# Latent attention taken four sequences at a time, values moved inside a loop, and filler matrix products before the norms of an eight-stage tower

## The chip, the cores and the metric

The kernel runs on one core of one Trainium2 chip. The metric is the device time of one execution in microseconds (us). Engines are named as the profile names them: PE is TensorE (matrix products), PEld its weight loads, DVE VectorE, ACT ScalarE, POOL GpSimd, SP the engine that here only issues DMAs. "PEq" and the like are an engine's own sequencer, mostly a barrier.

## The reference, cut to what matters

32 images become 32 sequences of 37 tokens of 256 features, and eight stages follow. Each stage is normalised first; the stages touched here are the first attention (L0_attn), the last one (latent attention, in L3_ffn), and the norms of all stages.

```
# L3_ffn, latent attention: 16 heads of 64, of which 32 without and 32 with rotation
q = (x @ Wq).reshape(b, t, H, D).transpose(0, 2, 1, 3)
ckv = x @ Wkva
kv_latent, k_rope = (ckv[:, :, :R], ckv[:, :, R:])
kv = (kv_latent @ Wkvb).reshape(b, t, H, NOPE).transpose(0, 2, 1, 3)
...
att = jnp.einsum('bhqd,bhkd->bhqk', q, k) / jnp.sqrt(jnp.float32(D))
att = jnp.where(mask, att, jnp.float32(-jnp.inf))
att = jax.nn.softmax(att, axis=-1)
y = jnp.einsum('bhqk,bhkd->bhqd', att, v)
# L0_attn, 16 heads of 16
out = jnp.einsum('bhqk,bhkd->bqhd', attn, V).reshape(B, S, H * dv)
```

A token attends only to earlier tokens of its own sequence.

## The kernel before

1184 tokens lie in 11 tiles of 111 rows (three sequences each; the last tile has two), `h` [111, 11, 256]. Each stage is one or more blocks. In a block each engine has its own program, written out in order; the engines meet only at semaphores, and at a barrier at the block's end, which also waits until an engine has issued all its DMAs. The order of the work is the order in which it is written; no planner sets it.

**Norms.** `norm_dve` (or `norm_transpose`) forms mean and variance of 11 tiles on DVE, POOL the power -0.5, DVE and ACT the normed tiles. PE waits for these (`norm_turn`, L1321; in `norm_transpose` L188) and turns them with 22 transposes into PSUM, from where ACT and DVE copy them into `xT`. Nine norms have such transposes: ap (attention 0), g, e, sn, mn, dn, de, lp (latent attention), le.

**Attention 0** (`stage_attn0`, L428). A first block forms queries, keys and values. Values leave PE in six pieces (L565). ACT copies queries to `qm` (16 copies, L607), then the values to `vt` (L614), and SP moves `vt` to `vx` by 24 DMAs (L505): 12 for tiles 0 to 3 once two pieces are there, 12 for the rest. A second block loops over 22 half-tiles: scores, softmax, transposes, mixing with `vx`, output.

**Latent attention** (`latent_attention`, L3704). The first block folds weights on PE (L3779), norms, and forms keys and eight query blocks as nine jobs: PE (L3797), ACT out of PSUM (L3839, L3841), DMA swap, and three DVE operations for the rotation (L3900, L3895, L3896). After job 4, eleven transposes give the values `lat` by tiles of 111 rows (L3811, copied at L3859 and L3861). The second block loops over 22 units of one tile (three sequences) and eight heads. The scores of a unit are 111x111 for each head, so two thirds of them join tokens of different sequences and are masked by `neg` [111, 111]. In steady state, for unit u:

- PE: 8 products of scores (L3936), 4 of mixing unit u-3 (L3959), 2 of the output of unit u-4 (L3970), 8 transposes of unit u-2 (L3948).
- DVE: mask added on the way out of PSUM (L4038), maximum (L4043), its negative times the scale (L4045); reciprocal of the sums and product with it (L4053, L4055); every second unit the output added to `r` (L4062).
- ACT: 8 exponentials with the maximum as bias and the sum as a second output (L3995), 2 copies of turned weights (L4007), 1 of mixed values (L4017).

A product of fp32 operands goes to PE as two instructions, a transpose as one. So 24 instructions are 12 products.

Of the kernel before, what the change touches and what calls it, by code (L numbers as in the profile page):

```python
# [15 lines left out]
ALU = mybir.AluOpType  # L16
# [7 lines left out]
P = 128  # L24
B, S, D = 32, 37, 256
G = 3
# [69 lines left out]

def norm_transpose(nc, name, h, xT, ident, eps, center, w_dram=None, w_plus=0.0, x_tok=None, turn=True,
# [5 lines left out]
    with ExitStack() as stack:  # L103
# [84 lines left out]
        def _(pe):  # L188
            for g, (a, b) in enumerate(groups):
# [238 lines left out]
def stage_attn0(nc, d, h, xT, ident):  # L428
# [7 lines left out]
    with ExitStack() as stack:  # L436
# [6 lines left out]
            "loop_in k_in v_in0 v_in1 v s_mm sc max exp norm turned pT mix oT out h").split()))  # L443
# [9 lines left out]
        bo = sb("a_bo", [1, D])  # L453
        ones = sb("a_ones", [1, TT])
        k_dram = nc.dram_tensor("a_kd", (D, G * SEQ), F32, kind="Internal").ap()

        with ExitStack() as inner:
# [10 lines left out]
            vt = sb2("ap_vt", [TT, NT, 2, NP, 2, 16])  # L468
# [8 lines left out]
            def _(sp):  # L477
# [22 lines left out]
                for m, (lo, hi) in enumerate(((0, 4), (4, NT))):  # L500
                    sp.wait_ge(n["values"], 2 if m == 0 else 6)
                    for q in range(G):
                        for a in range(2):
                            for x, y in ((0, 32), (32, S)):
                                sp.dma_start(  # L505
                                    vx[a * S + x:a * S + y, lo:hi, q, :, :].rearrange("j t p x -> j t (p x)"),
                                    vt[q * S + x:q * S + y, lo:hi, a, :, :, :].rearrange("j t p b x -> j t (p b x)")
                                ).then_inc(s[f"v_in{m}"], 16)

            @block.gpsimd  # L510
            def _(pool):
# [6 lines left out]
                nc.gpsimd.memset(vt[:, :, :, :, :, :], 0.0).then_inc(n["zero_v"], 1)  # L518

# [60 lines left out]
            def _(act):  # L580
# [20 lines left out]
                act.wait_ge(n["zero_q"], 1)  # L601
                for c in range(KC):
                    act.wait_ge(n["qu"], NCH * (c + 1))
                    for p in range(4):
                        for q in range(2):
                            dst, src = moved(c, p, q)
                            nc.scalar.activation(dst, src, ACT.Copy)  # L607
                act.wait_ge(n["zero_v"], 1)
                for m in range(6):
# [50 lines left out]
        with ExitStack() as inner:  # L660
# [3576 lines left out]
```

## Time and profile before

| | |
|---|---|
| three runs | 2040.03, 2045.87, 2044.94 us, median 2044.94 |
| the profiled execution | 2042.88 us, of which the span 2041.0 us |
| busy: PE, PEld, DVE, ACT, POOL | 71%, 56%, 72%, 42%, 30% |
| granted TensorE clock, mean | 0.84 of full |

The span lies between the first and the last instruction; 1.9 us lie around it. The granted clock is 1.00 (2.4 GHz) or 0.50 (1.2 GHz); means lie between. Where an engine's row says "idle before", the arrow names what ended the idle time.

### The profile page before, as it was taken

How to read it: one execution, taken by the hardware profiler on the slowest of the kernel's cores; microseconds unless marked ns; L12 is line 12 of the kernel's file. 1: busy time of each engine (PE TensorE's matmuls, PEld its weight loads, DVE VectorE, ACT ScalarE, POOL GpSimd, SP SyncE). 2: the span in 40 equal slices, each digit the busy share in tenths (PEclk: the TensorE clock that was granted, in tenths of full speed). 3: DMA queues.
4: the chain of work that ended last, by engine and by line, in shares of the span. 5: the costliest groups of instructions: out<-in, count | busy, mean ns of one | idle time of the engine just before them, and what ended most of it. 6: DMA issues, size and time to landing. Idle time of an engine off the chain costs nothing. (4 is left out here: it accounts for less than half of the span.)

```text
span 2041.0 us, 23929 instructions
## 1 busy us (share of the span) xinstructions
PE 1440.9 (71%) x8142; PEld 1134.0 (56%) x8142; DVE 1460.6 (72%) x2433; ACT 866.2 (42%) x1905; POOL 602.6 (30%) x395
## 2 busy tenths in 40 slices
PE   3678222469997825787657970797768889778797
PEld 3466101359997412344346970795347779556687
DVE  7566777898665459999945753687976466789576
ACT  5456230355552344554412530673233243369532
POOL 1400002122220028999805305125212141100310
PEclk9888555779999868898967995799889979889799
DMA  3410100111100003422045612101343010310110
GB/s 94 102 29 2 42 0 0 50 48 42 42 1 29 0 3 141 131 63 69 0 151 128 186 58 49 27 19 36 103 124 83 19 39 16 81 25 1 40 32 25
DMA packets 65583, 108.80 MB, mean 53 GB/s; under 512 B 34684, under 2 KB 43927, under 8 KB 63850
## 3 DMA queue, kind: packets, MB, share of 16 engines
q1 hardware_dynamic: 57725, 93.44, 15.7%
q0 software_dynamic: 6176, 8.84, 2.2%
q10 hardware_dynamic: 1562, 5.00, 0.8%
q8 instruction: 65, 1.06, 0.2%
q14 instruction: 55, 0.45, 0.1%
HBM read 83.85 MB, written 18.13 MB: 50 GB/s over the span
## 5 line engine op out<-in xcount | busy, mean ns | idle before, releaser
L2478 PE MATMUL c_pc<-c_st,ident 128*128 128x407 f32 x384 | 157.0, 559 | 49.4 <-POOL c_st L2441 42.2
L2433 POOL TENSOR_TENSOR c_dbub<-c_dub,c_bcb 128x814 f32<-128x814 f32 x96 | 169.5, 1788 | 16.4 <-DMA c_bcb<-s_bc 9.4
L2417 ACT ACTIVATE c_da<-s_delta,s_a 128x407 f32<-128x407 f32 x192 | 108.1, 594 | 115.1 <-DVE c_st L2525 100.2
L2478 PEld LDWEIGHTS c_pc<-c_st,ident 128*128 128x128 f32 x384 | 77.2, 208 | 127.7 <-POOL c_st L2441 59.0
L2521 DVE TENSOR_TENSOR_SCAN c_da<-c_da,c_dbub 128x814 f32<-128x814 f32 x60 | 110.6, 1843 | 1.7 <-POOL c_dbub L2433 1.7
L2019 ACT ACTIVATE e_sg<-e_pu,e_b 128x444 f32<-128x444 f32 (+1 forms) x96 | 56.6, 590 | 80.1 <-PE e_pu L1945 74.5
L2100 DVE TENSOR_TENSOR e_sg<-e_sg,e_gate 128x444 f32<-128x444 f32 (+1 forms) x96 | 54.7, 570 | 47.9 <-ACT e_sg L2019 44.7
L3172 DVE SCALAR_TENSOR_TENSOR dc_acc<-dc_pp,dc_cw,dc_acc 128x1311 f32<-128x1311 f32 x48 | 75.9, 1584 | 17.1 <-ACT dc_acc L3105 15.2
L1907 POOL TENSOR_TENSOR e_wlb<-e_wb,e_whb 128x1024 fp32r<-128x1024 f32 x16 | 42.1, 2657 | 125.8 <-ACT e_whb L1994 125.8
L2707 POOL DMA_INDIRECT me_xe<-m_xs,mt_rowsb x48 | 48.2, 1003 | 77.4 <-DVE mt_rowsb L2873 36.7
L2441 POOL TENSOR_TENSOR c_st<-c_st,c_bcb 128x814 f32<-128x814 f32 x36 | 68.6, 1906 | 4.6 <-DVE c_st L2518 4.6
L3368 POOL TENSOR_TENSOR do_msb<-do_msb,d_half 111x8 f32<-111x8 f32 x11 | 27.7, 2519 | 138.7 <-DVE do_msb L3629 138.7
L3995 ACT ACTIVATE la_eb<-la_scb,la_nmx 111x111 f32<-111x111 f32 (+1 forms) x176 | 66.5, 447 | 3.1 <-DVE la_nmx L4045 3.1
L1943 PE MATMUL e_pu<-e_xhb,e_wlb 128*128 128x444 f32 (+1 forms) x192 | 66.9, 348 | 1.1 <-ACT e_sg L2019 1.1
L2518 DVE TENSOR_TENSOR_SCAN c_st<-c_da,c_dbub 128x814 f32<-128x814 f32 x36 | 66.4, 1843 | 0.0
L1944 PE MATMUL e_pu<-e_xlb,e_whb 128*128 128x444 f32 (+1 forms) x192 | 65.8, 343 | 0.0
L1945 PE MATMUL e_pu<-e_xhb,e_whb 128*128 128x444 f32 (+1 forms) x192 | 65.8, 343 | 0.0
L1966 PE MATMUL e_acc<-e_hl,e_whb 128*128 128x444 f32 (+1 forms) x192 | 65.7, 342 | 0.0
L1968 PE MATMUL e_acc<-e_hh,e_whb 128*128 128x444 f32 (+1 forms) x192 | 65.7, 342 | 0.0
L1967 PE MATMUL e_acc<-e_hh,e_wlb 128*128 128x444 f32 (+1 forms) x192 | 65.7, 342 | 0.0
L2525 DVE TENSOR_TENSOR c_st<-c_da,c_bcb 128x814 f32<-128x814 f32 x60 | 60.4, 1006 | 2.1
L753 ACT ACTIVATE a_e<-a_m,a_nmx 111x37 f32<-111x37 f32 x176 | 48.5, 313 | 28.5 <-DVE a_nmx L804 28.4
(679 smaller groups left out, 4718.6 us busy)
## 6 DMA issues: line engine op xcount, KB each, us to landing
c_bcb<-s_bc SPq DMA_DIRECT2D x48, 407.0 KB, 4.1
m_wb<-in_m_w SPq DMA_DIRECT2D x16, 768.0 KB, 7.4
e_wb<-in_e_w SPq DMA_DIRECT2D x4, 2048.0 KB, 7.9
m_ys<-me_yb SPq DMA_DIRECT2D x16, 384.0 KB
d_z<-d_first ACTq DMA_DIRECT2D x11, 384.0 KB, 2.7
d_first<-d_z SPq DMA_DIRECT2D x11, 384.0 KB, 3.4
le_wb<-in_l_w_e SPq DMA_DIRECT2D x9, 384.0 KB, 3.0
de_wb<-in_d_w_e SPq DMA_DIRECT2D x8, 384.0 KB, 3.1
```

The source lines that it names most:

```text
L1943: nc.tensor.matmul(dst, w_lo, x_hi, start=(k == 0), stop=False)
L1944: nc.tensor.matmul(dst, w_hi, x_lo, start=False, stop=False)
L1945: last = nc.tensor.matmul(dst, w_hi, x_hi, start=False, stop=(k == KC - 1))
L1966: nc.tensor.matmul(dst, w_hi, h_lo, start=(e == 0 and f == 0), stop=False)
L2417: last = nc.scalar.activation(da[k % 2][:, c * CH:(c + 1) * CH], delta[:, t, c0 + c, :], ACT.Exp, scale=a[:, n, c0 + c:c0 + c + 1])
L2433: nc.gpsimd.tensor_tensor(wide(dbu[k % DB][:, :]), du[:, t, c0:c0 + HC, :], bc[n][:, 0:1, :].broadcast_to([P, HC, CH]), ALU.mult).then_inc ...
L2441: nc.gpsimd.tensor_tensor(one, one, bc[n][:, 1:2, :].broadcast_to([P, HC, CH]), ALU.mult).then_inc(s["c_pool"], 1)
L2478: last = nc.tensor.matmul(pc[:, c, 0:CH], ident[:, :], st[k % YB][:, c * CH:(c + 1) * CH], start=False, stop=(n == N - 1), skip_group_chec ...
L2518: nc.vector.tensor_tensor_scan(st[k % YB][:, :], da_k, dbu[k % DB][:, :], 0.0, ALU.mult, ALU.add).then_inc(s["c_vec"], 1)
L2521: nc.vector.tensor_tensor_scan(da_k, da_k, dbu[k % DB][:, :], 0.0, ALU.mult, ALU.add).then_inc(s["c_scan"], 1)
L3172: ins = nc.vector.scalar_tensor_tensor(one, pp[u][:, :, k:k + RUN], cw[:, ORDER[c], k:k + 1], one, ALU.mult, ALU.add)
L3995: last = nc.scalar.activation(e[0:R, u % 3, a, j, 0:R], sc[0:R, u % 2, a, j, 0:R], ACT.Exp, scale=HD ** -0.5, bias=nmx[0:R, u % 2, i:i + 1 ...
```

## The change

1. `warm` is a loop of matrix products of the identity with itself, 128x128, results unused. Twelve stand before the transposes of eight norms, 4 before those of latent attention, 16 at the end of PE's program in latent attention's first block.
2. Attention 0: ACT copies the first two pieces of values before its last four copies of queries. Of the 24 DMAs, 6 are issued by SP and 6 by POOL in the first block; the other 12 by SP in the second, where mixing waits for them at unit 8.
3. Latent attention's loop takes units of four sequences (8 units). Of the 8 query blocks of one sequence, three lie side by side as 111 rows, and only the sequence's own 37 keys are multiplied. The queries are laid out by sequences, the values `lat` as 37 rows of each sequence, twice (rows 0 and 64), by 32 small transposes. The maximum is subtracted on DVE, one exponential covers a unit, and DVE forms the sums. The table `l_neg` becomes [111, 37], and the order of heads in `layout_mla` changes.

```diff
+def warm(nc, out, ident, times):
+    for _ in range(times):
+        nc.tensor.matmul(out, ident[:, :], ident[:, :], start=True, stop=True)
...
+def norm_turn(nc, pe, s, xn, ident, at, filled=12):
+    warm(nc, at(0, 0)[:, 0:P], ident, filled)
...
-                for m, (lo, hi) in enumerate(((0, 4), (4, NT))):
-                    sp.wait_ge(n["values"], 2 if m == 0 else 6)
...
+                sp.wait_ge(n["values"], 2)
+                move_values(sp, 0, 4, (0,), s["v_in0"])
...
+                pool.wait_ge(n["values"], 2)
+                move_values(pool, 0, 4, (1,), s["v_in1"])
...
+                        if c == 1 and p == 2:
+                            act.wait_ge(n["zero_v"], 1)
+                            values(0)
+                            values(1)
...
+            @block.sync
+            def _(sp):
+                move_values(sp, 4, NT, (0, 1), s["v_in2"])
...
-        q = sb("l_q", [P, C, TV])
+        q = sb("l_q", [P, B * C * S + S])
-        lat = sb("l_latb", [TT, NT, LAT])
+        lat = sb("l_latb", [HD + S, B, LAT])
...
+                norm_turn(nc, pe, n, xn, ident, lambda g, k: pt[:, KC * g + k, :], 4)
...
+                pe.wait_ge(n["lat"], 1)
+                warm(nc, pm[:, 0, 0:P], ident, 16)
...
+                def scores(u):
                     if u >= 2:
                         pe.wait_ge(s["sc"], u - 1)
+                    for i in range(4):
+                        b = 4 * u + i
+                        for g in range(NG):
+                            for a in range(2):
+                                at, lo = slice(a * HD, (a + 1) * HD), b * C * S + g * TT
+                                last = nc.tensor.matmul(
+                                    psS[0:TT, u % 2 * 2 + a, (i * NG + g) * S:(i * NG + g + 1) * S], q[at, lo:lo + TT],
+                                    kx[at, b * S:(b + 1) * S], start=True, stop=True)
...
+                def mix(b):
+                    for e4 in range(2):
                         for a in range(2):
+                            at = (2 * a + e4) * LAT
+                            last = nc.tensor.matmul(
+                                psM[at:at + LAT, i * GG * S:(i + 1) * GG * S], lat[a * HD:a * HD + S, b, :],
+                                pT[a * HD:a * HD + S, b % 2, e4 * GG * S:(e4 + 1) * GG * S], start=True, stop=True)
...
+                scores(0)
+                scores(1)
+                turn(0)
+                turn(1)
+                for b in range(B):
+                    if b % 4 == 0 and b // 4 + 2 < U:
+                        scores(b // 4 + 2)
+                    mix(b)
+                    if b + 2 < B:
+                        turn(b + 2)
+                    if b % G == G - 1 and b >= 2 * G - 1:
+                        project(b // G - 1)
...
+                exps(0)
+                weights(0)
+                weights(1)
+                exps(1)
+                for b in range(B):
+                    if b + 2 < B:
+                        weights(b + 2)
+                    if b % 4 == 2 and b // 4 + 2 < U:
+                        exps(b // 4 + 2)
+                    if b % G == G - 1 or b == B - 1:
+                        mixed(b // G)
...
+                softmax(0)
+                normed(0)
+                softmax(1)
+                normed(1)
+                for b in range(B):
+                    if b % 4 == 0 and b // 4 + 2 < U:
+                        softmax(b // 4 + 2)
+                    if b % G == G - 1 and b >= 2 * G - 1:
+                        add(b // G - 1)
+                    if b % 4 == 3 and b // 4 + 2 < U:
+                        normed(b // 4 + 2)
```

`psS` has one bank for each half a of the rows, `psM` is one bank. POOL sets the new `e` to zero at the start of the loop (111x3072), since only 37 of every 64 columns are written.

The first place where rows move is the end of attention 0's first block. On ACT (`ap_qc`, `ap_pb`: queries, and PSUM with the values), before:

```order
L599 ACTIVATE ap_qc<-ap_pb,ap_uv 128x444 x2
L599 ACTIVATE ap_qc<-ap_pb,ap_uv 128x333
L607 ACTIVATE a_qm<-ap_qc 32x11x37 x16
L614 ACTIVATE ap_vt<-ap_pb 111x2x8x16 x10
L614 ACTIVATE ap_vt<-ap_pb 111x8x16 x2
```

and after the change:

```order
L612 ACTIVATE ap_qc<-ap_pb,ap_uv 128x444 x2
L612 ACTIVATE ap_qc<-ap_pb,ap_uv 128x333
L636 ACTIVATE a_qm<-ap_qc 32x11x37 x12
L621 ACTIVATE a_vtb<-ap_pb 111x2x8x16 x4
L636 ACTIVATE a_qm<-ap_qc 32x11x37 x4
L621 ACTIVATE a_vtb<-ap_pb 111x2x8x16 x6
```

Four copies of values went ahead of four copies of queries. On SP, after the change, the end of the first block and the start of the second:

```order
L470 DMA a_vx<-a_vtb 32x4x256
L470 DMA a_vx<-a_vtb 5x4x256
L476 UNCONDITIONAL_BRANCH
L698 UNCONDITIONAL_BRANCH
L470 DMA a_vx<-a_vtb 32x7x256
L470 DMA a_vx<-a_vtb 5x7x256
```

The branches are the step from block to block. Six DMAs of the shapes 32x4x256 and 5x4x256 stand ahead of it on SP and six on POOL, twelve behind it; before, all 24 stood ahead of it on SP.

The second place is PE in the loop of latent attention (`la_psS` scores, `la_psM` mixed values, `la_psO` output, `la_psT` turned weights). One unit before:

```order
L3936 MATMUL la_psS<-l_kx,l_q 111x111 x8
L3959 MATMUL la_psM<-la_pTb,l_latb 32x222 x4
L3970 MATMUL la_psO<-l_wvo,la_oTb 111x256 x2
L3948 MATMUL la_psT<-ident,la_eb 111x111 x8
L3936 MATMUL la_psS<-l_kx,l_q 111x111 x8
```

and two sequences after, from the scores of a unit on:

```order
L3966 MATMUL la_psS<-l_kx,l_q 111x37 x24
L3991 MATMUL la_psM<-la_pTb,l_latb 32x148 x4
L3979 MATMUL la_psT<-ident,la_eb 101x111 x3
L3991 MATMUL la_psM<-la_pTb,l_latb 32x148 x4
L3979 MATMUL la_psT<-ident,la_eb 101x111 x3
L4003 MATMUL la_psO<-l_wvo,la_oTb 111x256 x4
```

Scores now come in one run of 24 small products for each four sequences, and mixing and turning alternate by single sequences.

## Rows read from the trace of the kernel before

**Rows 1.** The end of attention 0's first block and its loop's start, in order of time.
```profile
81.97 7.29 ACT L607 ACTIVATE a_qm<-ap_qc 32x407 f32<-32x407 f32 x13
89.26 2.30 ACT L614 ACTIVATE ap_vt<-ap_pb 111x256 f32<-111x256 f32 x8
...
90.49 19.45 SPq L505 DMA_DIRECT2D a_vx<-ap_vt  x24
...
92.86 0.44 ACT L614 ACTIVATE ap_vt<-ap_pb 111x128 f32<-111x128 f32 x2 [0.20 <-PE ap_pb L565]
110.92 0.99 PE L688 MATMUL a_psS<-a_kx,a_qm 96*111 96x74 f32 x4 [18.10 <-PEq L457]
...
114.80 0.47 DVE L798 TENSOR_TENSOR a_m<-a_psS,a_band 111x296 f32<-111x296 f32 x1 [21.74 <-PE a_psS L691]
...
117.63 0.52 PE L688 MATMUL a_psS<-a_kx,a_qm 96*111 96x74 f32 x4
...
118.52 0.52 PE L688 MATMUL a_psS<-a_kx,a_qm 96*111 96x74 f32 x4
```
**Rows 2.** Instructions by line or tile: duration min/median/max in ns, first and last start.
```profile
L2707 POOL DMA_INDIRECT me_xe<-m_xs,mt_rowsb x48: 940/946/2284, 1083.4 to 1171.3; - x48
L4062 DVE TENSOR_TENSOR l_r<-l_r,la_psO x11: 410/414/421, 1829.8 to 1905.3; 111x256 f32<-111x256 f32 x10, 74x256 f32<-74x256 f32 x1
```
**Rows 3.** The loop of latent attention, in order of time, in its steady state.
```profile
1850.46 1.12 PE L3970 MATMUL la_psO<-l_wvo,la_oTb 128*111 128x256 f32 x4
...
1851.42 0.94 PE L3948 MATMUL la_psT<-ident,la_eb 111*111 111x111 f32 x8
...
1852.29 1.03 PE L3936 MATMUL la_psS<-l_kx,l_q 64*111 64x111 f32 x16
...
1853.13 1.08 DVE L4055 TENSOR_TENSOR la_eb<-la_eb,la_total 111x888 f32<-111x888 f32 x1
1853.77 0.45 ACT L3995 ACTIVATE la_eb<-la_scb,la_nmx 111x111 f32<-111x111 f32 x1
1854.00 0.58 PE L3959 MATMUL la_psM<-la_pTb,l_latb 111*32 111x222 f32 x8 [0.68 <-ACT la_pTb L4007]
```
**Rows 4.** The same loop by stretches: PE, PEld, DVE, ACT, POOL busy (instructions), clock, DMA, GB/s.
```profile
1846.00:1856.00 10.00, 8.58 (x88) 6.39 (x89) 9.26 (x15) 10.00 (x50) 0.00 (x0) 1.00 0.00 1
```
**Rows 5.** Latent attention's first block and its loop's start, in order of time.
```profile
1752.73 3.44 PE L3779 MATMUL lp_pm<-lp_wkb,lp_wqT 128*128 128x128 f32 x16 [9.42 <-DMA lp_wo<-in_l_wo]
...
1756.01 2.25 PE L1332 MATMUL lp_pt<-ident,lp_xn 111*128 111x111 f32 x22
...
1786.47 1.39 DVE L3900 TENSOR_TENSOR l_q<-lp_raw,lp_tab 128x1184 f32<-128x1184 f32 x1 [0.64 <-ACT lp_raw L3841]
...
1789.20 0.91 ACT L3839 ACTIVATE lp_raw<-lp_pt 128x888 f32<-128x888 f32 x1 [1.78 <-PE lp_pt L3797]
...
1806.23 4.53 PE L3936 MATMUL la_psS<-l_kx,l_q 64*111 64x111 f32 x48 [9.11 <-PEq L3727]
1808.10 1.08 DVE L4038 TENSOR_TENSOR la_scb<-la_psS,l_negb 111x888 f32<-111x888 f32 x1 [2.19 <-PE la_psS L3936]
```
**Rows 6.** PE alone, in order of time, where latent attention's loop begins.
```profile
1816.78 1.83 PE L3936 MATMUL la_psS<-l_kx,l_q 64*111 64x111 f32 x16
```
**Rows 7.** The norm before attention 0, in order of time.
```profile
52.77 0.43 DVE L1266 BATCH_NORM_STATS2 ap_stats<-h 111x6 f32<-111x256 f32 x1 [1.26 <-PEq L1251]
...
58.34 4.46 PE L1332 MATMUL ap_pb<-ident,ap_xn 111*128 111x111 f32 x22 [7.36 <-DVE ap_xn L1291]
...
59.43 1.38 DVE L1291 TENSOR_SCALAR ap_xn<-h,ap_mv,ap_rstdb 111x256 f32<-111x256 f32 x4
...
62.84 0.45 ACT L584 ACTIVATE xT<-ap_pb 128x333 f32<-128x333 f32 x1 [0.56 <-PE ap_pb L1332]
```
**Rows 8.** Stretches of one microsecond around that norm; the clock stands third from the end.
```profile
55.00:56.00 1.00, 0.00 (x0) 0.00 (x0) 0.97 (x9) 0.00 (x0) 0.34 (x1) 0.92 0.76 244
62.00:63.00 1.00, 1.00 (x6) 0.85 (x5) 0.51 (x1) 0.44 (x2) 1.00 (x1) 0.67 0.00 0
```

More of the change, by code:

```diff
@@ L600, in _, with values @@
                                              bias=uv[:, 0, c:c + 1]).then_inc(n["qu"], 1)
[L601 to L609, printed above, removed]
+                def values(m):
                     act.wait_ge(n["mm"], 18 + m + 1)
@@ new lines, in scores, with turn @@
+                    last.then_inc(s["s_mm"], 1)
+                def turn(b):
+                    u, i = divmod(b, 4)
+                    pe.wait_ge(s["norm"], u + 1)
+                    if b >= 2:
+                        pe.wait_ge(s["pT"], b - 1)
+                    for g in range(NG):
+                        src = e[:, u % 2, i * NG + g, :, :].rearrange("p a j -> p (a j)")[:, 0:HD + S]
+                        last = nc.tensor.transpose(psT[0:HD + S, b % 2, g * TT:(g + 1) * TT], src, ident[0:TT, 0:TT])
+                    last.then_inc(s["turned"], 1)
@@ L3961, in mix, with project @@
                     last.then_inc(s["mix"], 1)
-                def project(u):
-                    R, t, half = rows(u), u // 2, u % 2
-                    pe.wait_ge(s["oT"], u + 1)
-                    if half == 0 and t:
+                def project(t):
+                    R = seqs(t) * S
+                    pe.wait_ge(s["oT"], t + 1)
+                    if t:
                         pe.wait_ge(s["h"], t)
-                    for a in range(2):
-                        last = nc.tensor.matmul(psO[0:R, 0:D], oT[:, half, a * R:(a + 1) * R], wvo[:, 2 * half + a, :],
-                                                start=(half == 0 and a == 0), stop=(half == 1 and a == 1))
+                    for k in range(GG):
+                        last = nc.tensor.matmul(psO[0:R, 0:D], oT[:, t % 2, k, :, :].rearrange("p s j -> p (s j)")[:, 0:R],
+                                                wvo[:, k, :], start=(k == 0), stop=(k == GG - 1))
@@ L3984, in _ @@
+                for t in range((B - 1) // G - 1, NT):
+                    project(t)
             @block.scalar
@@ L3998, in exps @@
-                    last.then_inc(s["exp"], 1)
-                def weights(u):
-                    R = rows(u)
-                    if u >= 2:
-                        act.wait_ge(s["mix"], u - 1)
-                    for a in range(2):
-                        act.wait_ge(s["turned"], 2 * u + a + 1)
-                        nc.scalar.activation(pT[0:R, u % 2, a, :, 0:R],
-                                             psT[0:R, a, 0:4 * R].rearrange("p (j t) -> p j t", t=R), ACT.Copy
-                                             ).then_inc(s["pT"], 1)
@@ L4011, in mixed @@
-                def mixed(u):
-                    R = rows(u)
-                    act.wait_ge(s["mix"], u + 1)
-                    if u >= 2:
-                        act.wait_ge(s["out"], u - 1)
-                    nc.scalar.activation(oT[:, u % 2, 0:2 * R], psM[:, 0:2 * R], ACT.Copy).then_inc(s["oT"], 1)
-                for u in range(U + 4):
-                    if 0 <= u - 3 < U:
-                        mixed(u - 3)
-                    if 0 <= u - 2 < U:
-                        weights(u - 2)
-                    if u < U:
-                        exps(u)
+                    if u == 0:
+                        act.wait_ge(s["zero"], 1)
@@ new lines, in mixed @@
+                def mixed(t):
+                    k = seqs(t)
+                    act.wait_ge(s["mix"], t * G + k)
+                    if t >= 2:
+                        act.wait_ge(s["out"], t - 1)
+                    nc.scalar.activation(oT[:, t % 2, :, 0:k, :].rearrange("p g s j -> p s g j"),
+                                         psM[:, 0:k * GG * S].rearrange("p (s g j) -> p s g j", g=GG, j=S), ACT.Copy
+                                         ).then_inc(s["oT"], 1)
+                exps(0)
@@ L4101, in layout_mla @@
     o["l_wkva"] = cols(np.concatenate([wkva, wkva], 1), KC)
-    heads = np.array([[8 * (g // 2) + 2 * j + g % 2 for j in range(4)] for g in range(4)])
+    heads = np.array([[8 * (j % 2) + 2 * g + j // 2 for j in range(4)] for g in range(4)])
     o["l_wqT"] = wq[:, heads, 0:32].transpose(2, 3, 1, 0).reshape(P, 4, D)
```

191 lines of the change are left out of this document (85 added, 106 removed).

## The prediction

> **What bounds the kernel now.** I read the busy times first: PE 71%, DVE 72%. Neither engine is full, so every stage has to be read by itself, and I went to the three places that the change touches.
>
> First, in order of time, attention 0 between its two blocks. ACT's last copy of values ends at 93.3 us, yet PE's first product of the loop starts at 110.92, after 18.10 us of idle time ended by a barrier [rows 1]. Between them only SP is at work: 24 DMAs, issued from 90.49 for 19.45 us. So 17.6 us are nothing but the issue of DMAs.
>
> Second, the loop of latent attention. By stretches ACT is full (10.00 of 10) while PE has 8.58 and DVE 9.26 [rows 4]. It starts at 1806.23 [rows 5] and its last addition starts at 1905.3 and takes 0.41 [rows 2], so it takes 99.5 us, 4.5 for each of 22 units. Mixing waits 0.68 for ACT's copies [rows 3]. ACT is the bound, and eight exponentials with their bias and sum are most of what it does.
>
> Third, the norms. Before attention 0, PE sat idle for 7.36 us before its transposes at 58.34 [rows 7]. The granted clock fell about 55.8 (mean 0.92 in the microsecond from 55) and rose at 62.7 (0.67 in that from 62) [rows 8]: the transposes ran at 1.2 GHz, 22 in 4.46 us. In latent attention the same 22 follow other products, run mostly at 2.4 GHz and take 2.25 us [rows 5].
>
> **Moved values: 15.7 + 1.9 = 17.6 us won.** Four copies of queries at 7.29/13 = 0.56 us now stand behind the first values, which therefore start at 89.26 - 2.24 = 87.0 and, at 2.30/8 = 0.29 each, are done at 88.2 [rows 1]. SP issues six DMAs at 19.45/24 = 0.81: to 93.1. POOL issues six as well. The trace of before has no such DMA from POOL; its nearest row is a gather, 0.95 median and 2.28 at most [rows 2]. I take 1.0, by the median: to 94.2. ACT still ends at 93.3. The barrier cost 110.92 - (90.49 + 19.45) = 1.0, so the loop starts at 95.2, 15.7 earlier. Ends: 16.6 (POOL as fast as SP; ACT's 93.3 then decides) and 8.0 (2.28 each). The twelve late DMAs go out beside the loop, from 95 to 105, on an SP that has nothing else; mixing needs them at unit 8, some 36 us into the loop. Then the clock. The first DVE operation came 3.88 after the loop's start, with PE at 1.2 GHz; later half a unit of scores takes 118.52 - 117.63 = 0.89, so a unit 1.8 and the way to DVE about 0.2. After a pause of 2 us instead of 18 the clock should still be up: 1.9 won, ends 0 and 1.9.
>
> **Latent attention's loop: 99.5 becomes 81.** Prices per unit of four sequences, at 2.4 GHz:
>
> - PE, scores: 24 products are 48 instructions. They go in pairs on the two halves of the rows. At 1.2 GHz 48 took 4.53, 0.19 a pair [rows 5]; half of that, 0.097, I take at 2.4 GHz (8 pairs take 1.03 with the last one's end [rows 3]). I don't shorten it for 37 columns instead of 111, since each instruction still loads 111 columns of weights: in attention 0 four with 74 columns and 111 weights still take 0.52 [rows 1]. 24 pairs: 2.33.
> - PE, the rest: 3 transposes of a sequence 3 x 0.097 = 0.29 (8 take 0.94); 4 products of mixing 0.30 (those before, 222 columns against 148, take 0.58 with their end); an output 8 instructions, 2 x 0.87 = 1.73, once for three sequences [rows 3]. In all 2.33 + 4 x 0.59 + 1.33 x 1.73 = 7.0.
> - DVE: mask, maximum, subtraction, sum, product, all of 888 elements, 1.08 each (the rows of 888 elements in both [rows 3, 5]), a small reciprocal, about 0.2, and additions 1.33 x 0.41 [rows 2]: 6.2.
> - ACT: one exponential of 888 elements as the copy of 888, 0.91; four copies of 333 elements, 0.45 each [rows 7]; 1.33 copies of mixed values at about 0.58: 3.5. Before it had 4.5 for three sequences and half the heads, 12 for the same work. So ACT is no longer the bound.
>
> No engine's own sum is the unit's time, because the maximum, the exponential and the sum of a unit follow each other. I laid the four engines' programs out in their written order with these prices and 0.1 to 0.3 for each handover. DVE runs mask, maximum and subtraction (3.2), then waits for the exponential (0.9 and two handovers, more where ACT stands behind copies that wait for PE), then 2.4. With waits for outputs, masks stand 8.0 us apart. Head: 16.1 (scores 2.6, then two units at 6.7, no output yet). Six units at 8.0: 48.0. Tail: 11.5, mixing of the last sequences and four outputs of 1.73 with their handovers. Together 75.6. To this come 2.4, since scores of unit 0 then run at 1.2 GHz, as now (at that clock 16 take 1.83 instead of 1.03 [rows 5, 6]): the 16 filler products, 32 instructions in 3.4 us, end near 1803, five microseconds before the loop. And 3, for stretches in which PE's short bursts let the clock fall, from 0 (never) to 14 (half of the loop). 75.6 + 2.4 + 3 = 81, ends 75 and 95; 18.5 won.
>
> **Latent attention's first block: 1.5 lost.** PE goes from the fold (ends 1756.2) straight to its transposes, so four filler products are added to the path: the fold's 16 instructions took 3.44, mostly at low clock, 0.215 each; 8 at high clock 0.86 [rows 5]. 32 small transposes and two copies of 1024 elements (about 1.0 each by the 0.91 of 888) stand where eleven and two small ones stood; DVE already waited 0.64 for ACT's job behind them: 0.6. Ends 0 and 3. The new layout of the queries changes no element count.
>
> **Filler before eight norms: 3 won.** Twelve are 24 instructions, 2.6 at high clock and 5.2 at low. DVE's statistics and POOL's power take longer than that (7.4 from PE's last work to its transposes), so they delay nothing. What they can give: transposes of 2.25 rather than 4.46, but bound by the normed tiles, the last of which ends at 60.81 [rows 7]. That leaves 1.3 a norm. In attention 0 they would start with the block, as DVE's statistics do at 52.77 [rows 7], and end at 55.4, and 3 us of idle time remain before 58.34; before, 4.9 passed until the clock fell. I take one norm in three as kept, 8 x 1.3 / 3 = 3; ends 10 (all, with the products behind them) and -3 (the clock falls later and on dearer work). Here the transposes alone, from 58.34 to 62.4, preceded the rise. The Trainium skill says otherwise (TensorE: Matmul & The Clock Gate, Part 4): transposes don't count as activity. By that rule only the filler could lift the clock and the gain would be the 10; this trace speaks against it.
>
> **The sum.** -17.6 - 18.5 + 1.5 - 3 = -37.6. The profiled execution took 2042.9, 2.1 less than the median: 2005.3, rounded 2005. What a measurement tells from no change is 0.3%, 6 us.
>
> **The rivals.**
> - **Mixing goes one product after another.** Its four products use two halves of the rows and write one bank; before, mixing used all rows, and scores gave each half its own bank. 8 instructions one by one at 148 columns (0.12 each) are 1.0 instead of 0.30, 22 us over 32 sequences, of which some 15 show in the layout of the programs: 2020. Chance 15%. The Trainium skill has a rule for this (TensorEngine Tiling (Array Packing), Restrictions and Gotchas): different row tiles can't access the same PSUM bank at the same time. No row here shows such a case.
> - **POOL's DMAs at 2.28 each:** 2005 + 7.7 = 2013. 10%.
> - **The clock stays up** through the loop and most norms: 2005 - 5 - 7 = 1993. 12%.
> - **The loop stays at 1.2 GHz.** Scores at 37 columns feed PE thinly. PE then needs 8 x 4.7 + 32 x 1.2 + 11 x 3.4 = 113, with head, tail and handovers 124, and is the bound; the filler gives nothing: 2042.9 - 17.6 + 1.5 + 24.5 = 2051, slower by 0.4%. It decides above 122; before, the steady clock was 1.00 [rows 4]. 5%.
> - **The new loop is no faster than the old** (subtraction and sums on DVE eat it): 2024. 3%.
>
> The forecast itself has 55%. **How the numbers follow.** The range 1990 to 2024 holds the forecast's bounds and the rivals but the slow one and the ends of the others. Slower by over 0.3%: 0.04. Within 0.3%: 0.03. Faster: 0.93.
>
> **What would show it.** After: PE's idle time before attention 0's loop near 2 us instead of 18; the loop of latent attention some 81 us with the exponential once for each four sequences at about 0.9; DVE near 6 of 8 us a unit; eight starts of mixing products close together (a distance of 0.12 from one to the next would be the first rival). Wrong would be: a barrier that waits for POOL to 100 or later, DVE operations of 888 elements well over 1.08, or clocks of 0.50 over most of the loop.

## The result, and the profile after

| | before | changed |
|---|---|---|
| runs beside each other, us | 2040.03 to 2045.87, median 2043.31 | 2003.66 to 2015.12, median 2012.67 |
| ratio, 95% interval | | 0.9843 [0.9808, 0.9878] |
| the profiled execution, its span | 2042.88, 2041.0 | 2013.99, 2012.1 |
| granted clock, mean | 0.84 | 0.849 |

30.6 us faster where 37.6 were forecast; 2012.67 lies inside the range. By the profiled executions it is 28.9 us. I read the same places as before, in order of time.

**Attention 0's start** (answers to [rows 1]), in order of time:

```profile
87.04 13.08 SPq L470 DMA_DIRECT2D a_vx<-a_vtb  x11
87.33 3.67 POOL L470 DMA_DIRECT2D a_vx<-a_vtb  x6 [8.86 <-ACT a_vtb L621]
...
95.21 0.96 PE L713 MATMUL a_psS<-a_kx,a_qm 96*111 96x74 f32 x4 [3.58 <-PEq L476]
...
97.01 0.89 PE L713 MATMUL a_psS<-a_kx,a_qm 96*111 96x74 f32 x4
...
99.06 0.47 DVE L824 TENSOR_TENSOR a_m<-a_psS,a_band 111x296 f32<-111x296 f32 x1 [7.07 <-PE a_psS L716]
```

SP's row runs across the barrier: six of its DMAs come ahead of it. The loop starts at 95.21, where 95.2 was forecast, and PE waits 3.58 us for it instead of 18.10. But four score products take 0.96 and then 0.89 where 0.52 is the time at 2.4 GHz, and DVE comes 3.85 us after the start: the clock, up until 95.25, falls as the loop starts, and these products run at 1.2 GHz, as before.

**Norms**, PE's groups in the norm of the mixture of experts (mn), in the kernel before:

```profile
line engine op names shapes xcount | busy us, mean ns | idle before us <-releasers
L199 PE MATMUL mn_pt<-ident,m_x 111*128 111x111 f32 x22 | 4.5, 397 | 9.0 <-DVE m_x L167 9.0
```

and in the changed one:

```profile
L100 PE MATMUL mn_pt<-ident 128*128 128x128 f32 x24 | 4.4, 366 | 3.4 <-PEq L47 3.4
L207 PE MATMUL mn_pt<-ident,m_x 111*128 111x111 f32 x22 | 3.1, 271 | 1.2 <-DVE m_x L173 1.2
```

Here the filler ends 1.2 us ahead of the transposes, and they take 3.1 instead of 4.5. Where 2.7 us or more lie between, the gain is small or none: ahead of attention 0 the transposes still take 4.1 ([rows 7]: 4.46), and in the last norm (le) the first sixteen of the 22 keep their 3.3:

```profile
L1359 PE MATMUL ap_pb<-ident,ap_xn 111*128 111x111 f32 x22 | 4.1, 369 | 2.7 <-DVE ap_xn L1317 2.7
L100 PE MATMUL ap_pb<-ident 128*128 128x128 f32 x24 | 2.9, 278 | 1.8 <-PEq L1277 1.8
...
L1359 PE MATMUL le_po<-ident,le_xn 111*128 111x111 f32 x16 | 3.3, 399 | 3.3 <-DVE le_xn L1320 3.3
```

From PE's last product ahead of a norm to its first behind the transposes, the trace has, before and after: ap 11.62, 11.33; g 11.65, 11.24; e 41.40, 41.40; sn 17.10, 15.77; mn 17.51, 16.51; dn 68.25, 67.38; de 11.70, 11.64; le 12.00, 12.01. Together 4.0 us less. In e nothing is won although the filler ends 0.15 us ahead of the transposes: they take 14.3 us before and after, since PE waits 10.0 us among them for DVE's normed tiles.

**Latent attention's loop** by stretches, from its start at 1781.69: 0 to 5, 5 to 15, 15 to 22, 22 to 34, 34 to 59, 59 to 86 us (PE, PEld, DVE, ACT, POOL busy, clock, DMA share, GB/s; answers to [rows 4]):

```profile
1781.70:1786.70 5.00, 5.00 (x54) 5.00 (x56) 0.28 (x1) 1.28 (x1) 2.60 (x1) 0.50 0.00 0
1786.70:1796.70 10.00, 7.51 (x74) 7.16 (x72) 8.59 (x9) 2.00 (x4) 0.00 (x0) 0.50 0.01 2
1796.70:1803.70 7.00, 7.00 (x63) 4.97 (x61) 5.62 (x6) 1.72 (x3) 0.00 (x0) 0.50 0.00 0
1803.70:1815.70 12.00, 10.09 (x85) 7.96 (x85) 5.71 (x6) 3.51 (x7) 0.00 (x0) 0.50 0.00 1
1815.70:1840.70 25.00, 25.00 (x248) 17.23 (x247) 13.73 (x17) 8.10 (x16) 0.00 (x0) 0.80 0.00 1
1840.70:1867.70 27.00, 26.12 (x254) 18.08 (x251) 14.31 (x18) 8.14 (x17) 0.00 (x0) 0.81 0.01 2
```

```profile
1876.38 0.42 DVE L4104 TENSOR_TENSOR l_r<-l_r,la_psO 74x256 f32<-74x256 f32 x1 [2.10 <-PE la_psO L4003]
```

The last addition ends at 1876.8: 95.1 us where 81 were forecast and 99.5 stood. The clock is down for the first 37 us, then it falls three times more, each time within 0.7 us of the end of a run of 24 score products: 54 of the 95 us are at 1.2 GHz. ACT, full before, is busy under a third of the time; PE is now the bound. The groups of the low stretch (to 1818.5) beside single rows at high clock:

```profile
L3966 PE MATMUL la_psS<-l_kx,l_q 64*111 64x37 f32 x181 | 17.6, 379 | 0.0
L3979 PE MATMUL la_psT<-ident,la_eb 111*101 111x111 f32 x24 | 6.7, 426 | 2.5 <-DVE la_eb L4097 2.5
L3991 PE MATMUL la_psM<-la_pTb,l_latb 37*32 37x148 f32 x56 | 5.0, 450 | 1.9 <-ACT la_oTb L4049 1.9
```

```profile
1861.70 0.46 PE L3991 MATMUL la_psM<-la_pTb,l_latb 37*32 37x148 f32 x8
1862.09 0.53 PE L3979 MATMUL la_psT<-ident,la_eb 111*101 111x111 f32 x3
...
1865.10 1.89 PE L4003 MATMUL la_psO<-l_wvo,la_oTb 128*111 128x256 f32 x8
```

Mixing at high clock is 0.46 for eight instructions with the last one's end: they start in two fours, 0.006 apart within a four. DVE and ACT over the whole loop are near their prices, 1.08 as forecast and 0.96 beside 0.91:

```profile
L4080 DVE TENSOR_TENSOR la_mb<-la_psS,l_negb 111x888 f32<-111x888 f32 x8 | 8.6, 1078 | 9.8 <-PE la_psS L3966 9.8
...
L4031 ACT ACTIVATE la_eb<-la_mb 111x888 f32<-111x888 f32 x8 | 7.7, 959 | 5.4 <-DVE la_mb L4087 5.4
```

### The profile page after: what moved, and what is told of

It is laid out like the page before. It is cut to its first block and busy times, and to the rows that moved or that the text cites. A ratio compares the mean times of both kernels' runs of the same rounds, so it can differ in the third digit from the quotient of the medians.

```text
span 2012.1 us, 24043 instructions
## 1 busy us (share of the span) xinstructions
PE 1477.8 (73%) x8427; PEld 1166.1 (58%) x8427; DVE 1430.5 (71%) x2371; ACT 804.7 (40%) x1538; POOL 609.2 (30%) x403
## 3 DMA queue, kind: packets, MB, share of 16 engines
q1 hardware_dynamic: 57218, 92.96, 15.7%
## 5 line engine op out<-in xcount | busy, mean ns | idle before, releaser
L2496 PE MATMUL c_pc<-s_xc,c_dgb 128*128 128x407 f32 x24 | 15.5, 788 | 55.6 <-DVE c_dgb L2532 41.3
L2134 DVE TENSOR_TENSOR e_hl<-e_sg,e_hh 128x444 fp32r<-128x444 f32 (+1 forms) x96 | 54.2, 564 | 1.6
```

## The experiments

All ratios are to the kernel before, run beside them.

**Each part alone.** e1_moved: the kernel before with the moved values only. e2_norms: with twelve products ahead of eight norms only. e3_loop: with the new loop and its layout only, no filler. e4_no_filler: the changed kernel with

```diff
-                warm(nc, pt[:, 0, 0:P], ident, 12)
+                warm(nc, pt[:, 0, 0:P], ident, 0)
...
-def norm_turn(nc, pe, s, xn, ident, at, filled=12):
+def norm_turn(nc, pe, s, xn, ident, at, filled=0):
...
-                warm(nc, pm[:, 0, 0:P], ident, 16)
+                warm(nc, pm[:, 0, 0:P], ident, 0)
```

> The kernel before with the moved values alone. Theory A (the two traces): the whole shift of the start of attention 0's loop, 110.92 to 95.21, belongs to this part, less the 0.7 us by which token embedding happened to end earlier in the changed kernel's profile: loop start near 96, time 2028 us (2025 to 2031), PE's first product of the loop again at the low clock, about 0.96 for four score products instead of 0.52. Rival: part of that shift came from the filler before the norm; then the loop starts at 97 or later and the time is 2030 or more. In both the remaining pause before the loop is 2 us or more between the last DMA issue and the first product, and it is the barrier behind POOL's DMAs (about 1 us longer than before).

> The kernel before with the filler ahead of the eight norms alone (twelve products each; none in latent attention). Theory A: the filler is worth little: in the two traces the shift grows by 1.8 us over the norm at 653 to 670, 0.9 at 1039, 0.9 at 1284, 1.0 between 1913 and the end, and shrinks at others: 2 to 4 us faster, 2040 us. Rival B: it is worth the rest of what the parts don't explain (30.6 less 15.7 less 4.3 is about 10): 2033 us. Rival C: it is worth nothing, and what the traces show is the phase in which the clock falls and rises: 2043 us.

> The kernel before with latent attention's new loop, its layout and its small transposes, and no filler anywhere. Theory A (the new loop is bound by PE at 1.2 GHz): the loop takes 95 us or more from PE's first product to the last addition's end, where the old one took 99.5; with PE's wider start at low clock as before it is 93 to 99, and the time 2037 to 2043 us. Rival: the sixteen filler products made PE busy too early and their end let the clock fall on the loop; without them the loop is faster, 81 to 88 us, and the time 2025 to 2032 us.

> The changed kernel without any of its filler products (12, 4 and 16 become 0). Theory A: it is 1 to 4 us slower than the changed kernel, 2014 to 2017 us: the norms give up 2 to 4 and the fold gives back the 0.9 of four filler products. Rival B (the filler is worth about 10): 2022 us. Rival C (worth nothing): 2012 us or a little less. In all three the latent loop stays near 95 us, with long stretches at 1.2 GHz, since the filler ends six microseconds before it.

| | median us (before 2050.74) | ratio, interval | latent loop, us |
|---|---|---|---|
| e1_moved | 2035.97 | 0.9923 [0.9895, 0.995] | 97.0 (old) |
| e2_norms | 2045.41 | 0.9971 [0.9948, 0.9994] | 99.6 (old) |
| e3_loop | 2039.08 | 0.9944 [0.9925, 0.9962] | 88.8 |
| e4_no_filler | 2024.38 | 0.9878 [0.9847, 0.9909] | 88.9 |

The product of the first three is 0.9839, and the changed kernel has 0.9843: the parts add up, within intervals of some 4 to 6 us to each side. In us of 2043: values 15.7, norms 5.9, loop with its layout 11.4, in all 33.0 beside 32.1 for the changed kernel's ratio. Attention 0's loop in e1 starts at 95.72, as expected near 96, and at low clock (DVE 3.76 after it):

```profile
95.72 0.86 PE L705 MATMUL a_psS<-a_kx,a_qm 96*111 96x74 f32 x4 [3.78 <-PEq L468]
99.48 0.47 DVE L816 TENSOR_TENSOR a_m<-a_psS,a_band 111x296 f32<-111x296 f32 x1 [7.28 <-PE a_psS L708]
```

By e2 the filler is worth 5.9 us where I held 2 to 4, but the interval reaches from 1 to 11 us and doesn't exclude that; e4 without any filler is 0.35% above the changed kernel, 7 us, with intervals that overlap. The old loop itself took 97.0 us in e1 and 99.6 in e2: the clock fell at the loop's end, for 6.8 us, in e2 and not in e1. And for e3 and e4 I expected 93 to 99 us for the loop and found 89: by its length my rival (the sixteen products do harm) had it right, which the next set tries.

**The sixteen products ahead of the latent loop**: none in e5_lead0, 36 in e6_lead36.

> The changed kernel without the sixteen filler products ahead of latent attention's loop. The loop took 95.1 us in the changed kernel and 88.8 and 88.9 in the two kernels without any filler. Theory A (the sixteen products themselves make the loop slower, since the clock, up until 1781.4, falls at the loop's start and stays down for 37.6 us; without them it had fallen six microseconds earlier): the loop takes about 89 and the time is 6 us less than the changed kernel's. Rival B (only the moments at which the clock changes differ from program to program, and the sixteen have no part in it): the loop takes anything from 88 to 96 and the median of the runs moves by less than 3 us.

> The changed kernel with thirty-six filler products instead of sixteen ahead of latent attention's loop, so that PE is busy until about 1781.0, when DVE ends its last rotation, and has no pause before the loop. Theory A (the loop's own score products, 64 rows by 37 columns, are what the clock falls on): the clock is up for the first few microseconds (first masks some 2.4 us after the start instead of 4.7) and down from then on for 30 us as before; loop 90 to 95 us, time within 3 us of the changed kernel. Rival (the pause of 5.7 us before the loop made the clock fall and it cannot rise again): the clock stays up, the loop takes 76 to 82 us, and the time is 13 us or more below the changed kernel's.

e5: 2016.74 beside 2046.71, ratio 0.9842 [0.982, 0.9865], loop 89.0. e6: 2016.25, ratio 0.9843 [0.9818, 0.9869], loop 87.3. Both ratios are the changed kernel's, so the sixteen neither help nor harm by more than the some 5 us that the intervals leave open: for e5 theory A had the loop's length right and the 6 us of time wrong. Seven other profiles of the new loop without products inside it (e3 to e6, and e9, e11 and e12 below) have it at 87.0 to 89.1, with 34 to 39 us at low clock; the 95.1 of the changed kernel's, with 54, is the odd one. e6 is the telling one, PE in order of time and its first three microseconds:

```profile
1786.23 8.20 PE L100 MATMUL lp_pm<-ident 128*128 128x128 f32 x72
1795.51 4.83 PE L3966 MATMUL la_psS<-l_kx,l_q 64*111 64x37 f32 x80 [1.08 <-PEq L3754]
...
1825.55 0.88 PE L3979 MATMUL la_psT<-ident,la_eb 111*101 111x111 f32 x3
1826.22 3.46 PE L4003 MATMUL la_psO<-l_wvo,la_oTb 128*111 128x256 f32 x8
1829.61 0.46 PE L3991 MATMUL la_psM<-la_pTb,l_latb 37*32 37x148 f32 x8
1830.00 0.53 PE L3979 MATMUL la_psT<-ident,la_eb 111*101 111x111 f32 x3
```

```profile
1795.50:1798.50 3.00, 2.99 (x62) 3.00 (x63) 0.42 (x1) 0.29 (x1) 2.63 (x1) 1.00 0.02 5
1799.00:1804.00 5.00, 2.83 (x31) 2.69 (x30) 3.83 (x6) 1.46 (x2) 0.00 (x0) 0.50 0.00 0
```

The clock is up when the loop starts (first mask 2.57 us in, instead of 4.74), and falls 3.2 us later although PE had no pause from the loop's start on. Then it stays down for 30.7 us and rises at 1829.4, right behind the first output products that follow each other on all rows. In all eleven profiles of the new loop the rise at 33 to 41 us comes 1.4 to 4.4 us after the start of the first output. The Trainium skill (TensorE: Matmul & The Clock Gate, Why this matters for your kernels) advises no idle gaps of PE between bursts of products, so that the throughput doesn't drop. In this trace the clock dropped without such a gap, with PE busy 2.99 of 3.00 us before it.

In the old loop, though, the clock rose without an output. PE there in the kernel before, whose first output is at 1822.38:

```profile
1815.01 1.83 PE L3948 MATMUL la_psT<-ident,la_eb 111*111 111x111 f32 x8 [4.26 <-DVE la_eb L4055]
...
1822.38 1.12 PE L3970 MATMUL la_psO<-l_wvo,la_oTb 128*111 128x256 f32 x4
```

```profile
1806.30:1810.20 3.90, 3.90 (x42) 3.90 (x44) 2.06 (x2) 1.18 (x1) 0.00 (x0) 0.50 0.00 0
1810.40:1813.80 3.40, 0.35 (x8) 0.18 (x4) 2.50 (x5) 3.26 (x18) 0.00 (x0) 0.98 0.00 0
1814.10:1820.40 6.30, 5.39 (x37) 4.30 (x38) 6.00 (x8) 6.30 (x33) 0.00 (x0) 0.50 0.01 3
1820.60:1822.30 1.70, 1.70 (x28) 1.21 (x27) 1.63 (x5) 1.70 (x8) 0.00 (x0) 1.00 0.00 0
```

It rose at 1810.3 behind nothing but 4 us of score products of 64 rows and 111 columns, fell in PE's pause of 4.26 us, and rose again at 1820.5. In e1 the first of these rises is missing and the second comes at 12.4 us of the loop, also ahead of the first output at 15.8. So 64 rows alone don't keep the clock down; whether scores of 111 columns would have held it in the new loop was not tried.

**Filler inside the loop**: e7_inside, and e8_both with the 36 ahead as well.

```diff
                                     kx[at, b * S:(b + 1) * S], start=True, stop=True)
+                        if u < 2 and i < 3:
+                            warm(nc, psO[:, 0:P], ident, 1)
...
+                    warm(nc, psT[:, b % 2, 384:512], ident, 1)
                     for g in range(NG):
```

> The changed kernel with filler inside the latent loop: one product of the identity by itself between the sequences of the first two units of scores, and one ahead of each later sequence's transposes (30), into banks that TensorE holds at that time. Theory A (the low clock is the loop's whole excess over the forecast, and it is low because PE's own products of the first nine sequences, half the rows and 37 columns, do not hold it up): the clock rises within 10 us of the start and stays up but for short falls; the loop takes 80 to 85 us (75.6 laid out at high clock, 2.4 for the first scores, 2 to 7 for the filler and the rest), the time is 10 us or more below the changed kernel's. Rival: the clock is low whatever PE does in this loop; then 32 more products at 0.45 to 0.5 us make the loop 5 to 14 us longer, 100 us or more.

> Both of the two before: thirty-six filler products ahead of the loop, and one for each sequence inside. Theory A: the clock is up at the start and stays up; the loop takes 77 to 81 us, 15 us or so below the changed kernel's, time 1996 us beside 2012. Rival (the clock is low whatever PE does here): 100 us or more for the loop.

e7: 2027.97 beside 2046.71, ratio 0.9916 [0.9891, 0.9942], loop 99.7. e8: 2031.10, ratio 0.9899 [0.9872, 0.9927], loop 98.5. My theory, that one product for each sequence would lift the clock, fell in both: the clock was down for 40.6 us from the start in e7, and from 4.5 to 38.6 us in e8, and each product only cost its time (two of these instructions take 0.79 at low clock):

```profile
1788.85 1.34 PE L3966 MATMUL la_psS<-l_kx,l_q 64*111 64x37 f32 x12 [5.55 <-PEq L3754]
1790.12 0.79 PE L100 MATMUL la_psO<-ident 128*128 128x128 f32 x2
```

**Wider score products** (e9_wide) and **one solid piece of filler** (e10_burst):

```diff
+                                x, n = i * NG + g, 1 if b == B - 1 else 2
...
-                                    kx[at, b * S:(b + 1) * S], start=True, stop=True)
+                                    kx[at, b * S:(b + n) * S], start=True, stop=True)
```

```diff
                 scores(1)
+                warm(nc, psO[:, 0:P], ident, 14)
                 turn(0)
```

> The changed kernel with each score product of latent attention over 74 columns of keys (two sequences) instead of 37; the next product writes over the second half, so the result is as before, and the number of instructions and of weight columns too. Theory A (the granted clock falls on these products because they are thin): the clock stays up or rises within 15 us of the loop's start, a unit's scores at high clock take about 2.5 to 3.1 us, and the loop takes 80 to 88 us with at most 10 of them at low clock. Rival B (the low stretch belongs to the first 35 us of the loop whatever the score products look like, since PE has no output products there): low for 30 to 40 us as before, and the score products, if their time goes by columns of weights, still take 4.6 to 4.8 a unit: loop 88 to 96 us; if their time goes by moving columns too, up to 9 a unit and the loop 110 us or more.

> The changed kernel with fourteen filler products in one piece between the scores of the second unit and the first transposes of latent attention's loop. Theory A (a piece of back-to-back work over all rows lifts the clock, as the transposes before attention 0 did in 4 us, and the scores that follow drop it again): the filler starts at 1.2 GHz at 9.4 us and takes 4 to 6 us, the clock rises by 16 us, where it rose at 37.3, and falls again within 10 us; the loop's time 90 to 98 us. Rival (once up, the clock holds in this loop): it stays up from 16 us on, the loop takes 80 to 85 us. Second rival (the clock doesn't rise before 34 us whatever PE does): loop 100 us.

e9: 2011.13 beside 2041.74, ratio 0.9855 [0.9831, 0.988], loop 87.7, clock down for the first 35.4 us. Theory A fell: with 74 columns too the clock is down for the head of the loop. Once up it did not fall again in e9, where the other ten profiles of the new loop have at least one more fall; it is one profile, and the ratio shows no gain. The wider products cost next to nothing, 192 instructions in 18.8 us, 0.098 each, where 37 columns took 17.6 for 181, 0.097: their time doesn't go by the moving columns. That it goes by the weights is my reading; in the changed kernel PE's weight loads fill the loop's first 5 us.

```profile
L3967 PE MATMUL la_psS<-l_kx,l_q 64*111 64x74 f32 x192 | 18.8, 389 | 5.5 <-PEq L3754 5.5
```

e10: 2011.42, ratio 0.9865 [0.9832, 0.9898], loop 89.4. PE in order of time:

```profile
1792.87 6.14 PE L100 MATMUL la_psO<-ident 128*128 128x128 f32 x28
1798.85 0.73 PE L3979 MATMUL la_psT<-ident,la_eb 111*101 111x111 f32 x6
1799.51 2.53 PE L3966 MATMUL la_psS<-l_kx,l_q 64*111 64x37 f32 x48
...
1804.05 0.53 PE L3979 MATMUL la_psT<-ident,la_eb 111*101 111x111 f32 x3
1808.33 0.72 PE L3991 MATMUL la_psM<-la_pTb,l_latb 37*32 37x148 f32 x8 [3.75 <-ACT la_oTb L4050]
```

```profile
1798.80:1805.80 7.00, 5.78 (x89) 4.52 (x88) 4.65 (x6) 2.99 (x6) 0.00 (x0) 0.98 0.00 0
1805.80:1817.80 12.00, 9.47 (x83) 7.54 (x84) 6.63 (x7) 2.64 (x6) 0.00 (x0) 0.50 0.01 1
```

Theory A held for the clock, and its loop of 90 to 98 us is 89.4: 5.8 us of solid filler on all rows lift the clock at 14.9 us into the loop, a third unit's scores take 2.53 instead of 4.7, and the clock falls again at 21.7 us, after more thin products and as PE begins to wait for ACT. What is won in that stretch pays for the filler's 6.1 us and no more.

**Longer filler where the pause was left**, e11_norm22, and **all together with the DMAs split 8 and 4**, e12_all:

```diff
-                norm_turn(nc, pe, n, xn, ident, lambda g, k: pb[:, KC * g + k, :])
+                norm_turn(nc, pe, n, xn, ident, lambda g, k: pb[:, KC * g + k, :], 22)
...
+                pe.wait_ge(n["turn_read"], 6)
+                warm(nc, pb[:, 6, 0:P], ident, 11)
...
-            norm_turn(nc, pe, n, xn, ident, turned)
+            norm_turn(nc, pe, n, xn, ident, turned, 22)
```

```diff
+                move_values(sp, 0, 4, (1,), s["v_in0"], (2,))
...
-                move_values(pool, 0, 4, (1,), s["v_in1"])
+                move_values(pool, 0, 4, (1,), s["v_in1"], (0, 1))
...
-                warm(nc, pm[:, 0, 0:P], ident, 16)
+                warm(nc, pm[:, 0, 0:P], ident, 36)
```

> The changed kernel with twenty-two filler products instead of twelve ahead of the norms ap, g, de and le (where 2.7 to 3.3 us pass between the filler and the transposes), and eleven filler products after PE's last product of attention 0's first block (where 3.6 us pass before the loop). Theory A (a pause of about three microseconds at those four norms is what lets the clock fall on the transposes or right behind them, as the norms sn, mn and dn with pauses of 0.7 to 1.3 run at high clock): the 22 transposes of ap and g take 2.3 to 3.2 us instead of 4.1, attention 0's first DVE operation comes 2.0 us after the loop's start instead of 3.85: 3 to 7 us faster than the changed kernel, 2007 us beside 2012. Rival: the clock's changes come at moments that the filler does not move, the transposes are as fast or slow as before, and the time is the same within 3 us, or higher by up to 2 where the filler ends late at low clock.

> The kernel of e11_norm22 (twenty-two filler products ahead of four norms, eleven before attention 0's loop) with thirty-six products ahead of latent attention's loop, and with the twelve DMAs of attention 0's first values split 8 on SP and 4 on POOL instead of 6 and 6. In e11_norm22 POOL's DRAIN ran from 88.75 to 93.82, 3.9 us past the end of its last DMA issue, while SP's ended at 91.4 and PE's filler at 92.9, and the loop started at 94.25. Theory A (that DRAIN holds the barrier, and it ends some 3.9 us after POOL's last issue): POOL's ends at 92.6, SP's at 93.0, and the loop starts at 93.4, within 0.3. Rival (the barrier has a cost of its own whichever engine is last): it starts at 94.2 or later. Latent attention's first mask comes 2.6 us after the loop's start instead of 4.7, and the loop takes 87 to 88 us. In all 2 to 3 us below e11_norm22: a ratio to the kernel before of about 0.981, with a tie within 2 us as likely as not by the spread of the runs.

e11: 2004.00 beside 2041.74, ratio 0.9826 [0.9798, 0.9853]: 3.5 us below the changed kernel's ratio, but the intervals overlap, so the gain is seen in the trace and not clear in the time. PE ahead of le, and attention 0's start:

```profile
L100 PE MATMUL le_po<-ident 128*128 128x128 f32 x44 | 5.1, 277 | 1.6 <-PEq L1279 1.6
L1361 PE MATMUL le_po<-ident,le_xn 111*128 111x111 f32 x16 | 2.2, 274 | 1.0 <-DVE le_xn L1322 1.0
```

```profile
94.25 0.58 PE L715 MATMUL a_psS<-a_kx,a_qm 96*111 96x74 f32 x4 [1.39 <-PEq L476]
...
96.37 0.47 DVE L826 TENSOR_TENSOR a_m<-a_psS,a_band 111x296 f32<-111x296 f32 x1 [5.72 <-PE a_psS L718]
```

The first sixteen transposes of le take 2.2 instead of 3.3, ap's and g's twenty-two 3.1 instead of 4.1, and DVE comes 2.12 us after attention 0's start instead of 3.85. In e12 ap, g, de and le take 10.44, 10.48, 10.46 and 10.61 from product to product, 1.2 to 1.4 below the kernel before. A short pause is no guarantee: in e11 the clock fell within mn's transposes, 1.06 us behind their filler, and they took 3.9 us instead of 3.1.

e12: 2004.31 beside 2042.44, ratio 0.9813 [0.9785, 0.984]; a tie with e11 by the intervals. It beats the kernel before by 38 us. The changed kernel's ratio was 0.9843 [0.9808, 0.9878]: that e12 beats that one too is likely, but the intervals overlap. POOL's DMAs and the loop's start in e12:

```profile
86.62 2.57 POOL L470 DMA_DIRECT2D a_vx<-a_vtb  x4 [8.02 <-ACT a_vtb L624]
...
93.89 0.58 PE L716 MATMUL a_psS<-a_kx,a_qm 96*111 96x74 f32 x4 [0.52 <-PEq L476]
```

From SP's first issue to the loop's start it is 93.89 - 86.34 = 7.55 in e12 and 94.25 - 85.84 = 8.41 in e11: 0.86 less, as theory A has it (0.85); that the start is 93.89 and not 93.4 is the 0.5 by which e12 was already later at its first issue. The last to reach the barrier is POOL's DRAIN, the instruction that closes an engine's program in a block. It ends 3.9 us after POOL's last issue with six DMAs and 4.3 with four, where theory A had 3.9 for both; SP's DRAIN ends 0.07 ahead of it in e12, so a further shift from POOL to SP should win nothing (not tried). In all fourteen traces this loop starts 0.41 to 0.44 us after the last engine's DRAIN ends: SP's where it issues all 24, POOL's in the others. So the last DRAIN holds the barrier, as theory A has it, and the rival's 94.2 or later is out.

## Why the prediction was right, and where its sizes were off

- **Moved values, 15.7 forecast.** The mechanism is right (0.9923 in e1), but that the loop starts at 95.21 where 95.2 was forecast is luck: three errors cancel. POOL's first issue came 0.9 us earlier than laid out (87.33, not 88.2), for PE's first product of the block had come 1.2 earlier (61.44, not 62.61), only 0.3 of it by the filler; POOL's six DMAs took 3.67 us, not 6; and from its last issue to the loop 4.2 passed and not the 1.0 of the barrier, because the barrier waits for POOL's DRAIN. From the block's first product to the loop 14.5 us were won.
- **"After a pause of 2 us instead of 18 the clock should still be up: 1.9 won."** Wrong: the pause was 3.6 us and the clock fell at 95.25. The size was right: with filler in that pause e11 has 3.85 - 2.12 = 1.7 of it.
- **Latent attention's loop, 99.5 to 81.** Mechanism right, size wrong. The prices hold: exponential 0.96, DVE 1.08, mixing 0.46 and an output 1.89, both with their end, and with the clock up the last masks of e6 stand 9.1, 8.3 and 8.0 apart (8.0 forecast). What failed is the term "And 3, for stretches in which PE's short bursts let the clock fall, from 0 (never) to 14 (half of the loop)". In the profiles without products inside the loop the clock is down for 30 us or more of the first 35. e9's loop takes 87.7 us against 75.6 + 2.4, and in the changed kernel's own profile the excess is 17 and not 3, more than the 14 at which the term was to end (with it the sum reaches 92; the upper end of 95 has no working). Not all of the excess is the clock's: in e9 the masks of units 2, 4 and 7 come at 18.4, 40.8 and 66.3 us where the layout has 16.1, 32.1 and 56.1, so of its 12.1 us above 75.6 (2.4 of them forecast) 8.7 are there by unit 4, after the clock's rise at 35.4, and 3.4 come behind it with the clock up. The loop's gain is 11.4 by e3, with its layout, and 10.7 by that profile, not 18.5. I had laid out the head with the first scores alone at 1.2 GHz, and had not asked what holds the clock there. That the outputs, which the old loop has from its fifth unit on, held it in that one was my reading; its rises ahead of the first output speak against it, and the cause stays open.
- **First block, 1.5 lost.** From the end of the fold's last product to the loop's start it was 50.06 and is 51.09: 1.0. In e3, with the small transposes and no filler, it is 50.19, so they cost 0.1 and not 0.6, and the four filler products cost the forecast 0.9.
- **Filler, 3 won.** 4.0 by the eight norms in the two profiles, 5.9 [1, 11] by e2; three of eight (sn, mn, dn) kept the clock, "one norm in three" as I took it. The 10 by which only the filler could lift the clock is not borne out by the traces: in e4, with no filler, it rises behind the transposes of ap and le alone, as it did in the kernel before at ap.
- **Rivals.** Mixing goes in fours at once, not one by one at 0.12; the rule of the Trainium skill (TensorEngine Tiling (Array Packing), Restrictions and Gotchas), that row tiles can't access one PSUM bank at the same time, costs no time here: the halves write different partitions. POOL at 2.28 a DMA: 0.61. A clock that stays up: no. A loop all at 1.2 GHz: 54 of 95 us were in the changed kernel's profile, 32 to 39 of 87 to 89 in the others without a product for each sequence. So one of the signs that I had named as wrong, "clocks of 0.50 over most of the loop", did come true in the changed kernel's profile; and PE's idle time before attention 0's loop was 3.58 and not near 2.

By ratios the parts are 15.7 for attention 0 where 17.6 were forecast, 11.4 for the new loop with its layout where it was 18.5 - 1.5 = 17.0, and 5.9 for the norms where it was 3: in all 33.0 and not 37.6. The 30.6 between the medians agrees with that within the intervals. By the two profiles it is 15.7 at attention 0's start, 4.4 in latent attention's loop, 3.7 in the norms behind attention 0, less 1.0 in the first block: 22.8 of 28.9.

**Open.** Why the clock fell three times more in the changed kernel's profile (loop 95.1) and once or never in the others (87.0 to 89.4). Where the other 6 of the 28.9 us came from, between attention 0 and latent attention, in stages that the change leaves alone: two executions differ there by more than that (in e3, which shares them all with the kernel before, the shift between the two goes from 2.9 us earlier to 5.6 later within one stage of the experts, at 1098 to 1113 us). What PE would need in the head of the latent loop to hold the clock without paying for it; ACT's copy of mixed values stands there behind an exponential, and PE waits 3.75 us for it in e10. Another order of the two was not tried.

## What to carry to other kernels

When a change makes one engine's work thin (few rows, few columns, weights loaded for each product), price it at both clocks, and read from the old trace behind which products the clock rose and fell. Here the new loop spent most of its first 35 us at half speed, and the forecast had priced only its first scores so. Filler on an idle TensorE mostly paid here when it was one solid piece that ended 0.5 to 1.3 us ahead of the work behind it and that work did not wait for another engine, and it cost its full time when it was sprinkled between that work. DMA issues that a barrier waits for are worth moving behind it, and the barrier of this block ended with the last engine's DRAIN, not with the last issue.

## What the runs showed that I had not expected

- The clock fell with PE busy without a pause: e6, 3.2 us after its start, on score products of 64 rows and 37 columns. Doubling the columns (e9) changed neither the clock in the loop's head nor the products' time, 0.098 us each.
- It rose behind solid work on all rows: fourteen identity products, 28 instructions, from 9.1 us on (e10), or the first output at 31 to 34 us of the loop (e6). In the old loop it rose behind score products of 64 rows and 111 columns, with no output yet.
- POOL's DRAIN took 4.7 to 5.3 us behind four or six DMAs of its own queue, SP's 0.5.
